# Softmax reciprocals turned on TensorE, and the 8/norm scale moved from the exponential into the masking instruction

## The reference, cut to what matters

```python
q, k = l2norm(q) * qs, l2norm(k) * ksc        # 8 heads of 64
q, k = rotary_xpos(q, k)
sim = einsum(q * 8.0, k)                      # windows of 128, each sees itself and the one before
sim = where(mask, -max, sim)
attn = softmax(sim);  out = attn @ v
x = x + out @ wo
x = x + mlp(shift_token(x))                   # layernorm, gated gelu, 682 hidden
```

## Time and profile before

| | |
|---|---|
| median of 3 runs (lowest to highest) | 2963.74 us (2960.57 to 2964.81) |
| the profiled execution, its own time | 2961.57 us |
| span from its first to its last instruction | 2959.3 us, so 2.3 us lie around it |
| busy: PE, DVE, ACT, POOL | 2807.2, 2218.7, 2301.9, 1571.9 us |
| mean granted TensorE clock | 0.978 of full speed |

### The profile page before, as it was taken

How to read it: one execution, slowest core, us unless ns; L and a number is a source line. 1 busy time by engine, 2 the same in 40 slices (tenths; PEclk the granted TensorE clock), 3 DMA queues, 4 the chain that set the end, 5 groups by cost and what they waited for, 6 DMA issues and landing times.

```text
span 2959.3 us, 66953 instructions
## 1 busy us (share of the span) xinstructions
PE 2807.2 (95%) x22948; PEld 2536.5 (86%) x22948; DVE 2218.7 (75%) x6587; ACT 2301.9 (78%) x5301; POOL 1571.9 (53%) x1524
## 2 busy tenths in 40 slices
PE   7999938899999999999999999999999999999997
PEld 6878826788888889889898898899999999999987
DVE  3979967788777777887777676777777777777763
ACT  5989846788788878888887787788888888888873
POOL 2323225555656566566556555566666655666643
PEclk9999968999999999999999999999999999999998
DMA  3252112232323333323232335222222222222221
GB/s 97 63 186 70 38 57 48 48 52 47 55 51 53 48 53 55 54 45 54 51 54 45 76 55 92 46 48 48 48 48 48 50 47 49 47 48 47 50 39 34
DMA packets 342372, 166.19 MB, mean 56 GB/s; under 512 B 153618, under 2 KB 337684, under 8 KB 341012
## 3 DMA queue, kind: packets, MB, share of 16 engines
q1 hardware_dynamic: 342036, 161.93, 27.7%
HBM read 110.89 MB, written 42.58 MB: 52 GB/s over the span
## 4 chain that ended last, share of the span: by engine, by line
PE 59%; DVE 11%; DMA 10%; ACT 6%; issue 6%; POOL 5%; SPq 3%; DVEq 0%; ACTq 0%; POOLq 0%
PE ps L382 31%; PE ps L356 10%; DMA ro_scratch<-ro 7%; PE ps L466 4%; PE ps L452 4%; PE ps L440 4%; DMA oF<-ro_scratch 3%; PE ps L425 3%; ACT Sm L717 2%; POOL rs L1180 2%; DVE Sm L1034 2%; POOL r L1180 1%; DVE Gl L1107 1%; DVE oTl L1058 1%; DVE Ar L1007 1%
## 5 line engine op out<-in xcount | busy, mean ns | idle before, releaser
L717 ACT ACTIVATE Sm<-Sm,nb,sc 128x256 f32<-128x256 f32 (+1 forms) x1024 | 597.4, 586 | 2.2 <-DVE nb L1041 1.4
L1034 DVE CUSTOM_DVE_ANT_0 Sm<-ps,mask 128x256 f32<-128x256 f32 (+1 forms) x1024 | 368.0, 414 | 67.7 <-PE ps L440 65.5
L382 PE MATMUL ps<-zTh,W1h 128*128 128x256 f32 (+1 forms) x1408 | 407.2, 289 | 0.2
L382 PE MATMUL ps<-zTl,W1h 128*128 128x256 f32 (+1 forms) x1408 | 398.0, 283 | 0.2 <-issue 0.2
L382 PE MATMUL ps<-zTh,W1l 128*128 128x256 f32 (+1 forms) x1408 | 396.6, 282 | 0.0
L1180 POOL TENSOR_TENSOR rs<-rs,mhalf 128x16 f32<-128x16 f32 x128 | 372.3, 2908 | 0.0
L697 ACT ACTIVATE sq<-ps 128x512 f32<-128x512 f32 x256 | 152.6, 596 | 257.6 <-PE ps L382 252.7
L1266 POOL TENSOR_TENSOR uTl<-Gl,uTh 128x512 fp32r<-128x512 f32 (+1 forms) x192 | 211.8, 1106 | 260.3 <-ACT uTh L766 182.7
L382 PE MATMUL ps<-WQh,hTh 128*128 128x512 f32 x768 | 344.1, 448 | 3.3 <-DVE hTl L991 3.3
L1107 DVE SCALAR_TENSOR_TENSOR Gl<-ps,vecs,Gl 128x256 f32<-128x256 f32 (+1 forms) x384 | 170.5, 471 | 195.5 <-ACT Gl L756 100.0
L382 PE MATMUL ps<-WQl,hTh 128*128 128x512 f32 x768 | 306.3, 399 | 0.0
(11 more groups left out here) (184 smaller groups left out, 8650.9 us busy)
## 6 DMA issues: line engine op xcount, KB each, us to landing
oF<-ro_scratch SPq DMA_DIRECT2D x256, 128.0 KB, 3.4
tb<-tab SPq DMA_DIRECT2D x128, 128.0 KB, 2.6
xc<-x SPq DMA_DIRECT2D x32, 256.0 KB, 3.1
rwkv_scratch<-rw SPq DMA_DIRECT2D x32, 256.0 KB, 2.6
rk<-rwkv_scratch SPq DMA_DIRECT2D x64, 128.0 KB, 2.6
xin<-x SPq DMA_DIRECT2D x64, 128.0 KB, 2.4
x_scratch<-x SPq DMA_DIRECT2D x64, 128.0 KB, 2.6
y_scratch<-os SPq DMA_DIRECT2D x64, 128.0 KB
```

Source lines behind the costliest of these rows:

```text
L382: ins = pe.matmul(dst, L(a), R(b), start=start and i == 0, stop=stop and i == 2)
L717: act.activation(Sm[:, h, c0:c1_], Sm[:, h, c0:c1_], ACT.Exp, bias=nb[:, h:h + 1], scale=sc[:, n % 4, h:h + 1], accum_out=sm[:, n % 2, h:h ...
L1034: dve.tensor_tensor_reduce(Sm[:, h, c0:c1_], PS[:, bank["scores", n, q, h % 2], (h // 2 % 2) * 256 + c0:(h // 2 % 2) * 256 + c1_], mask[:, ...
```

## The change

`ro` is no longer stored transposed. It becomes single-buffered (128 x 8), PE turns it with one transpose into a PSUM bank of its own (8 x 128), ACT copies that to `r8` in SBUF, and the DMA stores eight rows of 512 bytes. `rT` is a new user in the ring of banks, between `qkv(t-2, 1)` and `qkT(t-3, 1)`; ACT's copy stands between `pre_norm` and `qk_hi(t-3, 1)`. In SP's list `store_r` moves from behind `shift` to right before `load_r`, behind the stores of the output and the reloads of weights. The masking instruction multiplies by `sc`, now -8/norm, and takes the minimum, which is the bias `nb` itself; the two small instructions per step that made `nb` go, and the exponential has the constant -1.0 as its scale in place of the operand `sc`.

```diff
@@ psum_order2
         yield "qkv", t - 2, 1
+    if live(5):
+        yield "rT", t - 5
     if live(3):
         yield "qkT", t - 3, 1
@@ tensor_program
+            def turn_r(n):
+                k = bank["rT", n]
+                w.wait_ge(S["ro"], n + 1)
+                w.wait_ge(*read_out(former["rT", n]))
+                pe.transpose(PS[0:8, k, 0:128], ro[:, :], ident[:, :]).then_inc(S["p7"], 1)
...
                 if live(2):
                     qkv(t - 2, 1)
+                if live(5):
+                    turn_r(t - 5)
@@ scalar_program
-                w.wait_ge(S["nb"], 2 * n + q + 1)
+                w.wait_ge(S["mx"], 8 * n + 4 * q + 4)
...
-                                   scale=sc[:, n % 4, h:h + 1], accum_out=sm[:, n % 2, h:h + 1]).then_inc(S["ex"], 1)
+                                   scale=-1.0, accum_out=sm[:, n % 2, h:h + 1]).then_inc(S["ex"], 1)
...
+            def rT_out(n):
+                w.wait_ge(S["p7"], n + 1)
+                w.wait_ge(S[f"sro{n % 2}"], 16 * (n // 2))
+                act.activation(r8[0:8, n % 2, :], PS[0:8, bank["rT", n], 0:128], ACT.Copy).then_inc(S["rT"], 1)
...
+                if live(5):
+                    rT_out(t - 5)
                 if live(3):
                     qk_hi(t - 3, 1)
@@ vector_program
+                w.wait_ge(S["sc"], n + 1)
+                w.wait_ge(S["ex"], 8 * (n - 1) + 4 * q + 4)
...
-                        mask[:, n % 2, c0:c1_], 1.0, -3.0e38, ALU.add, ALU.max, mx[:, h:h + 1]).then_inc(S["mx"], 1)
-                r = slice(4 * q, 4 * q + 4)
-                w.wait_ge(S["mx"], 8 * n + 4 * q + 4)
-                w.wait_ge(S["sc"], n + 1)
-                w.wait_ge(S["ex"], 8 * (n - 1) + 4 * q + 4)
-                dve.scalar_tensor_tensor(out=nb[:, r], in0=mx[:, r], scalar=-1.0, in1=sc[:, n % 4, r], op0=ALU.mult,
-                                         op1=ALU.mult).then_inc(S["nb"], 1)
+                        mask[:, n % 2, c0:c1_], sc[:, n % 4, h:h + 1], 3.0e38, ALU.add, ALU.min,
+                        nb[:, h:h + 1]).then_inc(S["mx"], 1)
...
-                w.wait_ge(S[f"sro{n % 2}"], 16 * (n // 2))
-                dve.reciprocal(ro[:, n % 2, :], sm[:, n % 2, :]).then_inc(S["ro"], 1)
+                w.wait_ge(S["p7"], n)
+                dve.reciprocal(ro[:, :], sm[:, n % 2, :]).then_inc(S["ro"], 1)
@@ gpsimd_program
-                pool.tensor_scalar(sc[:, n % 4, :], rs[:, n % 2, 0:8], 8.0, None, ALU.mult).then_inc(S["sc"], 1)
+                pool.tensor_scalar(sc[:, n % 4, :], rs[:, n % 2, 0:8], -8.0, None, ALU.mult).then_inc(S["sc"], 1)
@@ sync_program
-                w.wait_ge(S["ro"], n + 1)
+                w.wait_ge(S["rT"], n + 1)
                 w.wait_ge(S["on"], n - 3)
-                sp.dma_start(ro_d[n % 4].rearrange("h t -> t h"), ro[:, n % 2, :], allow_slow_non_contiguous=True).then_inc(S[f"sro{n % 2}"], 16)
+                sp.dma_start(ro_d[n % 4], r8[0:8, n % 2, :]).then_inc(S[f"sro{n % 2}"], 16)
...
-                if live(5):
-                    store_r(t - 5)
                 if live(12) and not odd:
                     store_out(t - 13)
                     store_out(t - 12)
...
                 if live(5):
+                    store_r(t - 5)
                     load_r(t - 5)
```

More of the change, by code:

```diff
@@ L255, in build @@
         Sm = sb("Sm", [8, 256])
-        mx = sb("mx", [8])
         sm = sb("sm", [2, 8])
@@ L259, in build @@
         PT = sb("PT", [8, 256])
-        ro = sb("ro", [2, 8])
+        ro = sb("ro", [8])
+        r8 = sb("r8", [2, 128])
         oF = sb("oF", [2, 4, 128])
@@ L296, in read_out @@
                 return S["x2"], n + 1
+            if what == "rT":
+                return S["rT"], n + 1
             if what == "zT":
```

## The result

The changed kernel takes 2929.03 us in the median of 4 runs (2927.88 to 2930.89), the kernel before 2962.15 in the same comparison (4 runs, 2959.57 to 2964.81). The ratio is 0.9889, 95% interval 0.9872 to 0.9906: 33 us or 1.1% faster. I had forecast 2962.7 and a range down to 2948. The case that I had called "faster, as the chain has it", with 2934 us and a chance of 0.05, came nearest in time, though its mechanism, the store slipping past the reloads, did not happen.

A forecast was written before the change was run, and what follows sets the result against it. PE was taken to bound steady phase 2, the round trip costing only in filling, change of layers and draining. Terms +7.0 - 1 + 0 - 5 - 9 + 7 = -1 us gave 2962.7 us; range over all cases 2948 to 2976.

The forecast's parts named there:

- faster, as the chain has it: Rival: store slips past the reloads and all 17.6 us at the change of layers go; about -30, 2934 us; chance 0.05.
- What bounds the kernel: Phase 2: PE bounds the steady layers; DVE's 155.4 us of waits overstate the round trip's cost by five or more.
- the three short places: Filling, change of layers and draining: where the reciprocals' DRAM round trip costs the kernel; forecast -5, +7 and -9 us.
- The transpose: PE, steady layer 1: each added transpose costs 0.11 us with nothing covering it; 64 make +7.0 us (0 to +17).
- the rival by the whole record of 0.27 us: PE: each of 128 transposes costs its full record in place of 0.11; +20, 2983 us; chance 0.03.
- The change of layers: Steps 65, 74, 75: the store now waits behind weight reloads; +3.3, +2 and +1.5, sum +7 us (0 to +12).
- The filling: Start of phase 2: PE's 7.9 us of waits for `o_norm` and `x2_out` shrink; -5 us (-8 to -2).
- The draining: End of phase 2: three successive round trips shorten by 2.5, 5 and 1.5 us; -9 us (-11 to -5).
- The store's own time: Reciprocals' store to DRAM: eight rows of 512 bytes land in 2.7 us (2.0 to 3.5).
- Steady layer 0: 26 pairs of steps: the latency chain through ACT to POOL's k gets 0.12 us shorter per pair; -1 us (-6.5 to +5.7).
- The ring: PSUM banks, layer 0: `pre` may wait for the `qkv` readout; counted 0; rival +12 us, 2974 us, chance 0.16.
- The masking instruction: DVE: reading `sc` lengthens it by 0 to 0.05 us, 0 to +0.4 us a step.

The follow-up runs named there:

- rows of 32 bytes: Kernel before, its store writing the reciprocals as they lie, 128 rows in place of 1024 elements, no transpose, output not the reference's: 2928.95 us, ratio 0.9839.
- the masking half: Only the new masking instruction and the exponential's constant scale, put on the kernel before: 2968.12 us against 2976.49, ratio 0.9979.
- the first half: Changed kernel with the old masking instruction, bias instructions and exponential put back; PE transpose, 512-byte rows, ring user and later store kept: 2932.68 us, ratio 0.9853.
- Taking that one neighbour away: Changed kernel with store and load ahead of the reloads, and `pre` moved ahead of `zT` in even steps: 2911.57 us against 2921.81 without the exchange.
- The same shift of banks: Empty ring user at `rT`'s place: on the kernel before 2961.89 us, with 32-byte rows 2923.24, with DVE's transpose and early store 2923.48 against 2899.80 without.
- the kernel without any: Changed kernel with store and load ahead of the reloads, reciprocals turned on DVE instead of PE, empty ring user kept: 2923.48 us, ratio 0.9864.

## Why the prediction was wrong

**What bounds the kernel** was read rightly. DVE's waits for `oF` fell from 155.4 to 18.0 us, of which 14.9 lie at the change of layers, and steady layer 1 gained next to nothing by a fast store (957.1 us with rows of 32 bytes, against 958.7). The error lies in the three short places and in the price of a wait there. That the case with a chance of 0.05 came nearest is luck: its own terms give -1 - 7 - 17.6 = -25.6 and not -30 us, and PE's waits at the change of layers fell by 10.2 of their 17.6 us only.

**The transpose**: +7.0 for 64 windows, so 5.7 for the 52 between the cuts, where the stage grew by 6.6. The doubled transpose gave 0.106 us for my 0.11: right, and the rival by the whole record of 0.27 us is refuted. The other 1.1 us came only with the masking half (965.3 us with it, 964.2 without), and its cause is open.

**The change of layers** is the step that failed, +7 forecast and -13.8 measured. I had written that the store behind the reload lands near where the reload ends and "only then the load goes out, another 4 us: +3.3". The order of the queue is as I said: 9.5 us pass before the load in step 65. What I took over unchanged was the length of the reload, 14.8 us. In the kernel before the reload stood behind 1024 packets of 4 bytes in the same queue; the store was issued here, and the load that waits for it went out at 1643.49, with the reload issued at 1639.17 in between:

```profile
1631.50 0.86 SPq L1420 DMA_DIRECT2D ro_scratch<-ro  x1
```

With 128 packets in their place the reload took 11.6 us, and with 8 packets, which stood behind it, 10.7; the W1 reload fell from 19.2 to 9.6 and 9.2. (Over the profiles WQ's took 13.1 to 14.8 us with elements and 10.2 to 11.6 without, W1's 19.0 to 19.9 and 9.0 to 11.1.) The element store was slow itself and held up what was queued behind it, the reloads and their waits included. In step 65 the two effects nearly cancel (DVE's wait 10.2 before, 9.0 after), in step 74 the wait went from 6.7 to 0.2, in step 75, where SP had needed 8.3 us to issue a part of W2's reload and then 1.6, from 10.1 to 5.7. Together PE's waits fell by 10.2 us, the clock gave 4.9 and 14 transposes took 1.5: -13.6. That the move costs was right, against the right reference: 10 us in the profiles, 7 to 8 in the medians, against the same kernel with the store ahead. (The Trainium skill, DMA: Bandwidth & Descriptors, "Rules for kernel authors", says that a strided last dimension becomes one descriptor per element; the packets here agree, 56389 under 512 bytes from 1900 to 2800 us before and 6577 after, which is (56389 - 6577) / 49 = 1017 fewer a window.)

**The clock** was priced nowhere. I took each wait of PE at its length, though my own table of the kernel before had a mean clock of 0.978. Each long wait was followed by work at 1.2 GHz, 2 to 3 us lost each time. At the change of layers 4.9 of the 13.8 us are this, in the filling 6.6 of the 9.1, where the waits themselves fell by only 1.8. The stalls that I put in show it as a mechanism: 22.9 us for 18.0 of waits.

**The filling**, -5 against -9.1: its waits were mis-sized by 3 and the clock left out. **The draining**, -9 against -9.9, came out near for a wrong reason: 7.9 us of waits and 6.3 of clock, less some 4 us more of PE's work at full speed between the cuts. That `o_norm` of window 124, no longer late, now marks an earlier place in PE's list would do that. The count of matmuls behind the cut, 729 before and 761 after, where 3 transposes were added, speaks for it.

**The store's own time** was mis-sized: 2.7 us taken, 1.2 measured from issue to the load's issue; on the steady path it is off PE's chain.

**Steady layer 0**, -1 (-6.5 to +5.7) against -5.8, is inside its bounds. It comes with the first half (1019.1 alone) and not with the exponential's 0.09 us an instruction, which came as forecast (0.590 to 0.497) and bought nothing there.

**The ring** I had counted at 0 and kept as a rival with +12 us, and said that waits at L382 for L1009 would speak for it. They came, at L386 in the new numbering:

```profile
PE ps L386 <- DVE Br L1028: 8.2, 24, 1.5
```

Yet they don't show that the new order as a whole cost time. Taking that one neighbour away gave 10 us. But a fast store with the old order made layer 0 longer (1028.2 us against 1024.7), and with the new one shorter (1021.3), so what layer 0 gained came with the new order beside a fast store. The changed kernel with the old order wasn't run. The same shift of banks was worth -2 (within the noise), -7 and +24 us in three surroundings. What decides that isn't settled: the twofold transpose made the wait shorter, the kernel without any made it longer, so the phase of PE against DVE's readout is in it, and that I can only argue.

**The masking instruction** costs DVE the full 0.05 and a little more (0.419 to 0.480 us), against two small instructions saved. That moved layer 0 by nothing and layer 1 by the 1.1 us above. The half as a whole was worth some 3 us beside the fast store, in medians from two chips, and 6 with the slow one.

## What to carry to other kernels

The DMA with an element per descriptor was paid for by everything queued behind it: price its packets on the queue's other users, and expect their lengths to change when it goes. A long wait of the bound engine costs its length and the slow stretch behind it (4.4 us on 12.9 here, nothing on two waits of 2.6), so take the granted clock into the sum wherever the table of windows shows less than 1.00. And when a user joins a ring of banks, compute who follows whom and measure it, as one exchange of two lines was worth 10 us here; the best version, turned on DVE with the old ring and the store ahead of the reloads, takes 2900 us, 2.1% under the kernel before.

## What of the hardware I had not expected

- The landing of a 4 KB store went by its packets: 11.1 us as 1024 of 4 bytes, 4.1 as 128 of 32 bytes, 1.2 as 8 of 512 bytes, from its issue to the issue of the load that waited for it (medians, steady layer 0).
- Two stalls of 2.6 us left the clock at 2.4 GHz; two of about 6.5 us were each followed by 6.8 us at 1.2 GHz, in which PE was busy for 3.4 and 5.2 us; by half of that the loss was 1.7 and 2.6 us, not 3.4 each.
- A transpose with 8 columns as weights starts the next instruction 0.11 us later, just as one with 128.
- The kernel with the element stores differed by 13 us between chips, 2963 and 2976.
